# A head worked batch by batch: one batch's gates and projections ahead of the other's

## The reference, cut to what matters

```python
xn = layernorm(x)                         # x: (2, 1024, 128)
def ffn(xn):                              # attention with low-rank experts
    pooled = xn.mean(axis=1)              # one row per batch
    logits = relu(pooled @ gw1.T + gb1) @ gw2.T + gb2
    gates  = softmax(top_k(logits, 2))    # 2 of 8 experts, per batch
    W[p]   = Wm[p] + sum_e gate_e * U[p,e] diag(S[p,e]) V[p,e]    # p in q, k, v, o
    q, k, v = xn @ W[q] * SCALE, xn @ W[k], xn @ W[v]             # 16 heads of 8
    return softmax(q k^T) v @ W[o]
def attn(xn):                             # RWKV: time mixing, then channel mixing
    h = layernorm(xn); k, v, r = mix(h) @ w_tk, mix(h) @ w_tv, sigmoid(mix(h) @ w_tr)
    x1 = xn + r * wkv(k, v)               # a scan over 1024 tokens
    return x1 + sigmoid(cr @ w_cr) * (relu(ck @ w_ck)**2 @ w_cv)
out = x + attn(xn) + ffn(xn)
```

## Time and profile before

| | |
|---|---|
| median of 3 runs | 448.7 us (448.13 to 449.81) |
| the profiled execution | 447.99 us, span of its instructions 445.9 us |
| busy share of the span | PE 95%, DVE 86%, ACT 76%, POOL 43% |
| mean granted clock of PE | 0.992 of full speed |
| first place of stage A | 30.91 us |
| scores of step 0 / of step 1 | 64.63 us / 67.31 us |

### The profile page before, as it was taken

The page is one execution under the profiler, slowest core; times in us unless marked ns, Lnnn a source line. Parts: engine busy times, 40 slices in busy tenths (PEclk is TensorE's granted clock), DMA queues, the critical chain, the costliest instruction groups (busy, mean ns, idle before and its releaser), DMA issues.

```text
span 445.9 us, 8560 instructions
## 1 busy us (share of the span) xinstructions
PE 423.2 (95%) x3248; PEld 144.7 (32%) x3248; DVE 385.4 (86%) x657; ACT 340.2 (76%) x461; POOL 191.2 (43%) x271
## 2 busy tenths in 40 slices
PE   1889989999999999999999999999999999999995
PEld 1644223333233232232323223323232333322334
DVE  8578899998999997899999789999888999976354
ACT  3547837879887898788799969878986877988660
POOL 5029581935551625382353546417264611431200
PEclk9988999999999999999999999999999999999999
DMA  7004303141414141404241413332322421050301
GB/s 240 11 11 56 40 6 34 19 66 21 64 22 67 20 66 18 64 7 70 24 64 19 66 17 54 31 60 24 60 27 26 57 37 28 17 116 10 124 25 47
DMA packets 45509, 20.46 MB, mean 46 GB/s; under 512 B 36796, under 2 KB 36956, under 8 KB 45468
## 3 DMA queue, kind: packets, MB, share of 16 engines
q1 hardware_dynamic: 44486, 18.96, 27.6%
q10 hardware_dynamic: 982, 0.95, 0.6%
HBM read 4.74 MB, written 4.98 MB: 22 GB/s over the span
## 4 chain that ended last, share of the span: by engine, by line
PE 86%; DVE 9%; ACT 3%; issue 1%; DMA 1%; DVEq 0%
PE banks L1475 27%; PE banks L1462 22%; PE banks L1365 18%; PE banks L1426 8%; DVE half_max L1177 5%; PE banks L1327 3%; ACT probs L972 2%; PE banks L1333 1%; PE banks L1405 1%; PE banks L1311 1%; PE banks L1262 1%; DVE work L1204 1%; PE banks L1319 1%; PE banks L1228 1%; DVE stats L1023 1%
## 5 line engine op out<-in xcount | busy, mean ns | idle before, releaser
L1177 DVE TENSOR_REDUCE half_max<-banks 128x1 f32<-128x512 f32 x512 | 318.5, 684 | 21.2 <-PE banks L1365 19.6
L972 ACT ACTIVATE probs<-banks 128x1024 f32<-128x1024 f32 x256 | 248.2, 1023 | 51.5 <-PE banks L1462 48.3
L1475 PE MATMUL banks<-probs,v_op 128*32 128x512 f32 x1024 | 136.4, 605 | 0.4 <-ACT probs L972 0.4
L1365 PE MATMUL banks<-k_main,q_main 64*128 64x512 bf16 x512 | 117.5, 388 | 5.6 <-DVE half_max L1177 3.3
L1462 PE MATMUL banks<-q_main,k_main 64*128 64x512 bf16 x512 | 99.3, 377 | 0.4 <-ACT probs L972 0.2
L1462 PE MATMUL banks<-q_tail,k_tail 35*128 35x512 bf16 x512 | 99.3, 377 | 0.0
L1365 PEld LDWEIGHTS banks<-k_main,q_main 64*128 64x128 bf16 x512 | 36.5, 93 | 151.0 <-DVE half_max L1177 132.1
L1462 PEld LDWEIGHTS banks<-q_tail,k_tail 35*128 35x128 bf16 x512 | 27.2, 94 | 26.1
L1462 PEld LDWEIGHTS banks<-q_main,k_main 64*128 64x128 bf16 x512 | 26.4, 95 | 25.1 <-ACT probs L972 10.2
L1475 PEld LDWEIGHTS banks<-probs,v_op 128*32 128x32 f32 x1024 | 20.1, 108 | 32.5 <-issue 30.3
L718 POOL TENSOR_TENSOR work<-work 128x512 f32<-128x512 f32 x16 | 16.6, 1039 | 28.6 <-ACT work L961 28.6
(11 more groups left out here) (184 smaller groups left out, 420.5 us busy)
## 6 DMA issues: line engine op xcount, KB each, us to landing
ctx_dram<-ctx_sb SPq DMA_DIRECT2D x15, 256.0 KB, 2.1
q_main<-parts SPq DMA_DIRECT2D x60, 48.0 KB
k_main<-parts SPq DMA_DIRECT2D x60, 48.0 KB
mat_sb<-in_mats_dram SPq DMA_DIRECT2D x2, 768.0 KB, 5.3
v_op<-V SPq DMA_DIRECT2D x16, 64.0 KB, 3.9
parts<-ctx_dram SPq DMA_DIRECT2D x4, 256.0 KB, 4.4
q_main<-parts SPq DMA_DIRECT2D x30, 32.0 KB
k_main<-parts SPq DMA_DIRECT2D x30, 32.0 KB
```

The costliest lines, as they stand in the source:

```text
L972: a.activation(probs[:, (2 * step + h) % 4, :, :], banks[:, 2 * h:2 * h + 2, :], ACT.Exp).then_inc(b_read, 1)
L1177: v.tensor_reduce(half_max[:, n % 2, u:u + 1], ring_bank(at), axis=AX.X, op=ALU.max).then_inc(a_read, 1)
L1365: mm(dst, q_main[HALF * e:HALF * (e + 1), s, P * c:P * c + P], k_main[HALF * e:HALF * (e + 1), s, CHUNK * h:CHUNK * h + CHUNK], start=True ...
L1475: last = mm(banks[g:g + 32, PV_BANK, :], v_op[:, s % 2, step, e, :], probs[:, (2 * step + h) % 4, e, :], start=(step == 0), stop=True, ski ...
```

## The change: what it does

**Head.** Only batch 0 is prepared. Chunks 0 and 1 are measured and normalised first, on DVE, and each tile is transposed as soon as it is there. Batch 0's gates are computed alone, on one partition, and only its q and k weights; chunks 2 and 3 are normalised on ACT (`normalise`, 8 tiles, with a bias and a scale per token) instead of DVE. Only q and k of the first 512 tokens (banks 0 and 2) are projected, split and laid out before the first place, and bank 3 is projected.

**Pair 0's places.** Their order goes by 512 columns of keys and then by queries, so that the first eight need only the first 512 tokens of q and k, the next eight bank 3 (k), the last sixteen bank 1 (q).

**Opening.** What the head no longer does is set between the places: the rest of bank 3, all of bank 1, batch 1's gate column, the v and o weights (`weights` 0 and 1) and q's and k's weights of batch 1 (`weights` 2). Three of the nine `mixed` jobs go to the main loop, which then has six. The transposes, `late` and `values` jobs are spread anew, and the banks are assigned by a table (`FILL_BANKS`).

**Other engines.** The scaling of U moves from DVE to ACT (six of eight), the 22 small copies into `row_of` from ACT to POOL, the copies of pair 0's rows all to ACT, the constants of chunks 2 and 3 to POOL. DVE adds the main weights between its reads (`ADD_WEIGHTS`). SP loads pair 1 before pair 0's tails. The kernel computes the same.

```diff
-FILL_JOBS = {2: [("turn", 0), ("turn", 1)], 5: [("turn", 2), ("turn", 3)], 9: [("values", 0)], 12: [("values", 1)]}
-FILL_JOBS.update({15 + 2 * m: [("mixed", m)] for m in range(6)})
-FILL_JOBS.update({26: [("late", 0)], 28: [("late", 1)], 30: [("late", 2)], 31: [("late", 3)]})
-FILL_JOBS.update({38: [("mixed", 6)], 40: [("mixed", 7)], 42: [("mixed", 8)]})
-LATE_JOBS = {2: ("mixed", 9), 3: ("mixed", 10), 9: ("mixed", 11), 10: ("values", 2), 15: ("values", 3)}
-LATE_GATES = {2: 2, 12: 3}
+FILL_JOBS = {0: [("gates", 1)], 2: [("left", 3, 0), ("turn", 0)], 4: [("left", 3, 1)], 5: [("rows", 3)], 7: [("project", 1)],
+             8: [("turn", 1)], 9: [("left", 1, 0)], 11: [("left", 1, 1), ("weights", 0)], 13: [("rows", 1)], 15: [("turn", 2)],
+             17: [("weights", 1)], 19: [("mixed", 0)], 21: [("mixed", 1)], 23: [("mixed", 2)], 25: [("turn", 3)],
+             27: [("values", 0)], 29: [("values", 1)], 31: [("mixed", 3)], 33: [("mixed", 4)], 34: [("mixed", 5)],
+             36: [("weights", 2)], 38: [("late", 0)], 40: [("late", 1)], 41: [("late", 2)], 43: [("late", 3)]}
+READ_GATES, ADD_WEIGHTS = 2, {13: ((2, None),), 19: ((3, None),), 37: ((0, 1), (1, 1))}
+LATE_JOBS = {2: ("mixed", 6), 4: ("mixed", 7), 7: ("mixed", 8), 10: ("mixed", 9), 12: ("mixed", 10), 15: ("mixed", 11),
+             18: ("values", 2), 20: ("values", 3)}
+LATE_GATES = {8: 2, 16: 3}
...
 # SP
-            load_tails(0, 0)
             load_pair(1, 1)
+            load_tails(0, 0)
...
 # ACT, up to the opening
+            scale_of(0); scale_of(1)
...
+            keep_xnT(0); keep_xnT(1)
+            hidden_gates(0)
+            scale_of(2); scale_of(3)
+            act.dma_start(vb_ob[:, :, :], ...)
+            exp_gates(0)
...
+            normalise(2); normalise(3)
...
+            keep_xnT(2); keep_xnT(3)
+            part(0, 0, 0); hidden_gates(1)
+            part(0, 0, 1); exp_gates(1)
+            part(0, 0, 2); keep_rows(0); keep_rows(2)
+            part(3, 0, 0); part(3, 0, 1); part(3, 0, 2)
+            keep_h(0); keep_rows(3); scale_shift(0)
+            part(1, 0, 0); scale_shift(1); keep_h(1); part(1, 0, 1)
+            scale_u(2, 0); scale_u(2, 1)
+            part(1, 0, 2); scale_shift(2); keep_rows(1)
...
 # DVE
+            part(2, 0, 0); top_gate(1); part(2, 0, 1); compare_gates(1); part(2, 0, 2); weigh_gates(1)
...
 # PE
+            hidden_gates(0); warm(6)
+            logits_of(0); warm(20)
+            for k in range(4):
+                pe.wait_ge(xn_late, k + 1)
+                turn_x(2, (k,))
+            gate_column(0)
...
+            turn_x(3, (0, 1))          # then the weights of q and k, batch 0, and turn_x(3, (2, 3))
+            project(0); project(2)
+            take_part(0, 0); hidden_gates(1); take_part(2, 0); take_part(0, 1); logits_of(1); take_part(2, 1)
+            pair_rows(0); pair_rows(2); project(3)
...
-                if n == 0 and k == 0:
-                    pe.wait_ge(q_rows_kept, 2)
-                    pe.wait_ge(k_rows_kept, 2)
+                if n == 0 and k in (0, 8, 16):
+                    pe.wait_ge(rows_kept, 2 + k // 8)
```

More of the change, by code:

```diff
@@ L745, in _ @@
             split_max(0, 0)
+            bias_v(1)
+            take_shift(3)
             mix_tokens(3)
@@ L778, in _ @@
             act.dma_start(gw2_sb[:, :], gw2).then_inc(small_in, 16)
[L779 to L788, removed]
@@ L789, in _, with scale_of @@
-            act.dma_start(vb_ob[:, :, :], rows.rearrange("(o r) c -> o r c", o=1).to_broadcast([P, 2, C])
-            ).then_inc(rows_in, 16)
+            act.dma_start(gb2_sb[:, :], gb2).then_inc(small_in, 16)
+            act.wait_ge(consts, 2)
+            def scale_of(n):
+                of_n = slice(4 * n, 4 * n + 4)
+                act.wait_ge(moments_ready, 4 * n + 4)
+                a.activation(rstd[:, of_n], moments[:, of_n, 1], ACT.Ln, bias=eps_c[:, 0:1]).then_inc(log_var, 1)
+                act.wait_ge(log_var, n + 1)
+                a.activation(rstd[:, of_n], rstd[:, of_n], ACT.Exp, scale=-0.5).then_inc(rstd_ready, 1)
@@ new lines, in keep_xnT, with normalise @@
+            def keep_xnT(n):
+                act.wait_ge(x_transposed, n + 1)
+                a.activation(columns_of(xnT, n), bank(n), ACT.Copy, accum_out=sums[:, n:n + 1]).then_inc(xnT_ready, 1)
+            def normalise(n):
+                act.wait_ge(late_shift, n - 1)
+                for i in range(4 * n, 4 * n + 4):
+                    a.activation(xn_tok[:, i, :], x_sb[:, i, :], ACT.Identity, bias=neg_mean[:, i:i + 1],
+                                 scale=rstd[:, i:i + 1]).then_inc(xn_late, 1)
@@ L794, in _ @@
             a.activation(col("qS"), col("qS"), ACT.Copy, scale=SCALE).then_inc(q_scaled, 1)
-            def keep_xnT(n):
-                act.wait_ge(x_transposed, n + 1)
-                a.activation(columns_of(xnT, n), bank(n), ACT.Copy, accum_out=sums[:, n:n + 1]).then_inc(xnT_ready, 1)
[L801 to L806, removed]
@@ L807, in _ @@
-            act.wait_ge(shifted_ready, 1)
-            a.activation(gexp[:, :], logits[:, :], ACT.Exp, bias=neg_top[:, 0:1]).then_inc(gexp_ready, 1)
-            act.wait_ge(var2_ready, B)
+            keep_xnT(0)
+            keep_xnT(1)
+            hidden_gates(0)
+            scale_of(2)
+            scale_of(3)
+            act.dma_start(vb_ob[:, :, :], rows.rearrange("(o r) c -> o r c", o=1).to_broadcast([P, 2, C])
+            ).then_inc(rows_in, 16)
+            exp_gates(0)
+            act.wait_ge(moe_in, 16)
@@ L815, in _ @@
[L815 to L825, removed]
+            a.activation(rstd2[:, :], rstd2[:, :], ACT.Exp, scale=-0.5).then_inc(rstd2_ready, 1)
@@ L834, in part, with keep_rows, scale_u @@
                              bias=col("kb") if t else qb_s[:, 0:1]).then_inc(part_ready[j], 1)
[L836 to L843, removed]
+            def keep_rows(j):
+                t, n = part_bank(j, 0)
+                act.wait_ge(rows_ps, ROW_ORDER.index(j) + 1)
+                a.copy((k_main if t else q_main)[:, 0, CHUNK * n:CHUNK * (n + 1)], bank(j)).then_inc(rows_kept, 1)
+            def scale_u(i, b):
+                act.wait_ge(sg_ready, 2)
+                a.activation(u_s[:, i, b, :], mat("qkvo"[i] + "U"), ACT.Copy, scale=sg[:, i, b:b + 1]).then_inc(us_ready, 1)
             def keep_h(u):
@@ L857, in keep_v, with scale_shift @@
                     "p (k r w) -> p k r w", k=CHUNK // P, w=2 * HD)).then_inc(v_read, 1)
[L859 to L864, removed]
+            def scale_shift(m):
+                act.wait_ge(h_diff, m // 3 + 1)
+                a.activation(mix_slot[m], h_shift[CHUNK_ORDER[m // 3]], ACT.Copy,
+                             scale=col("mix_" + "kvr"[m % 3])).then_inc(h_scaled, 1)
             def keep_kvr(m, src):
@@ L915, in _ @@
                           max_rows[80:96, 0, :]).then_inc(max_in[0], 16)
-            for m in range(6, 9):
-                keep_kvr(m, bank(kvr_bank(m)))
+            keep_kvr(5, bank(kvr_bank(5)))
+            keep_gate(1)
+            for m in (9, 10, 11):
+                scale_shift(m)
+            for j in range(CHUNKS):
+                keep_late(j)
             weights = ((lo_u, 1.0, 0.0), (hi_u, -1.0, 0.0), (lo_y, 1.0, neg_first[:, :]), (hi_y, -1.0, col("first")))
@@ L1186, in _ @@
                 read_place(at)
+                if at == READ_GATES:
+                    scale_gates(1)
+                for i, b in ADD_WEIGHTS.get(at, ()):
+                    add_main(i, b)
             def one_step(p, step):
@@ L1269, in take_part, with pair_rows @@
                    skip_group_check=True).then_inc(left_ps[j], 1)
+            def pair_rows(j):
+                t, n = part_bank(j, 0)
+                pe.wait_ge(part_ready[j], PARTS)
+                for i in range(PARTS):
+                    last = mm(bank(j), row_of[:, t, i, :], parts[0:2 * HD, t, i, n, :], start=(i == 0),
+                              stop=(i == PARTS - 1))
+                last.then_inc(rows_ps, 1)
+            for n in range(2):
+                for k in range(4):
+                    pe.wait_ge(xn_ready, 4 * n + k + 1)
+                    turn_x(n, (k,))
@@ L1271, in _ @@
+            pe.wait_ge(neg_ident_ok, 1)
+            warm(8)
+            pe.wait_ge(small_in, 64)
+            hidden_gates(0)
+            warm(6)
+            logits_of(0)
+            warm(20)
+            for k in range(4):
+                pe.wait_ge(xn_late, k + 1)
+                turn_x(2, (k,))
+            gate_column(0)
+            pe.wait_ge(xn_late, 8)
+            turn_x(3, (0, 1))
             pe.wait_ge(moe_in, 16)
-            expert_weights(0)
-            expert_weights(1)
@@ L1274, in _ @@
-            warm(4)
+            for i in range(2):
+                pe.wait_ge(us_first, i + 1)
+                mm(bank(5 + i)[:, 0:P], mat("qk"[i] + "V"), u_s[:, i, 0, :], start=True, stop=True).then_inc(weff_ps, 1)
+            turn_x(3, (2, 3))
             pe.wait_ge(weff_ready, 1)
             project(0)
```

(25 more changed lines are left out.)

407 lines of the change are left out of this document (226 added, 181 removed).

## The result

The change made the kernel slower: 453.25 us (median of 20 runs, 450.45 to 458.93) against 449.02 (20 runs, 448.13 to 451.33), a ratio of 1.0081 [1.0058, 1.0103]. The ratio leaves out the three slowest runs of the changed kernel (457.4 to 458.9), in which the mean clock was lowest. The forecast was 448.4, with 452.2 as the upper end. The profiled execution took 453.03.

What follows compares the result with a forecast made beforehand. PE was taken to carry most of the chain of waits. From the profiled 447.99, 4.9 saved up to step 1's scores and 4.6 lost in the loop gave 447.7, with the median 0.7 above: 448.4 us, range 444.4 to 452.2.

Steps and rivals of the forecast that it cites:

- The head: Work before the first place: `project(0)` at 16.6 instead of 20.17, first place at 24.7, 6.2 us earlier.
- The opening: From first place to step 1's scores: place 16 at 36.7, scores at 62.4, giving back 1.3 of 6.2 us.
- The walk: Place-by-place pricing of ACT's and PE's streams in the opening: 12.0 us for the first sixteen places.
- The sign "after 64": End of the opening: the prediction is wrong if step 1's scores come after 64.
- the sign for the clock: Head: PE's granted clock was to read 1.00 from 10 to 24.
- The third case: Half clock in the head, falling before about 17 us: 2.8 us more, 451.2; chance 0.14.
- Transposes don't feel it: Head and opening: transposes cost the same at half clock, 0.27 at full against 0.24 at half.
- The loop: Main loop gives back 4.6 us: 3.15 for three more `mixed` jobs, 1.1 for bare scans, 0.35 for `keep_gate(3)`.
- The 0.35 for `keep_gate(3)`: Main loop: cost of moving `keep_gate(3)` from step 12 to step 16, between nothing and 0.6.
- The wait ahead of `late 0`: Opening: PE waits 0.9 us before `late 0` for the two `add_main` behind place 37.
- The late maxima: Opening: SP starts 6 us later, so maxima land late for step 0's scores; 451.5, chance 0.08.
- The even case: Whole kernel: the head's gain is paid back by jobs and bare scans, 446.5 to 450.9; chance 0.45.

Runs made afterwards that it cites:

- experiment 1: Changed kernel plus identity products, whose result nobody reads, in PE's pauses in the head; 448.14 us, 0.9973 of the kernel before.
- experiment 6: Kernel of experiment 4 with only the move of three `mixed` jobs from the opening to the main loop; 454.6 us, ratio 1.009.
- experiment 3: Changed kernel with the layout matmuls over 128 rows instead of 16, added selector rows zero; 448.27 us, ratio 0.9989.
- experiment 4: Kernel before the change with the layout matmuls over 128 rows instead of 16; 446.93 us (0.9936), in a second run 447.45 us (0.9952).
- experiment 5: Kernel before the change without its 60 identity products; 452.82 us, ratio 1.0051.
- experiments 7 and 8: Changed kernel, identity products in the head, layout over 128 rows; 7: loop jobs on steps 3 and 9, 445.85 us; 8: three `mixed` back in opening, 445.18 us.

## Why the prediction was wrong

The forecast held in its main terms but for one step, and that step carried 6 us.

- **The head: right.** `project(0)` forecast at 16.6, measured 16.52, behind ACT's eight tiles (11.9 to 14.75; 11.87 to 14.95, 0.385 apart for 0.35). The gates' first matmul came at 9.68 (9.3). First place 25.16 (24.7); in it is 0.36 of a `project(3)` that took 1.42 instead of 1.06, since the clock fell in it.
- **The opening: the step that failed**, "place 16 comes at 36.7 ... 62.4, 4.9 earlier than 67.31". The walk priced every pass, turn and layout from 24.7 on at 2.4 GHz, while the earlier trace rows of the same argument showed 1.2 GHz behind just these layouts. Measured, place 16 came at 42.81 and step 1 at 68.73: all of the loss arises before place 16. With the clock held (experiment 1) place 16 came at 36.84 and step 1 at 62.81: the walk itself was right to 0.4, and what failed was the clock that its prices took for granted. The sign "after 64" is the one that came true; the sign for the clock ended at 24, just ahead of the fall.
- **The third case named the mechanism, at the wrong place and size.** It put the fall before about 17 us and charged 2.8 for four items of the head. The clock stayed up there: `project(0)` took 1.98 / 4 = 0.50 a pass. By the rule of the Trainium skill, "TensorE: Matmul & The Clock Gate", Part 4: PE-mode transpose, that thin stretch of transposes would have throttled; the trace shows no such fall, as those 0.50 tell, but the stretch is only some 4 us behind the last identity product and holds other passes too, so it doesn't settle the rule. The clock fell at 24.3, behind the thin stretch from 18 to 22 and the first layouts, and cost 68.73 - 62.81 = 5.9 in the opening. A chance of 0.14 was too small for something that the kernel before already did, and 451.2 was too near. Its counter-argument, full clock through as thin a stretch at 8 to 14, trusted a column that is wrong there (under the hardware, below).
- **"Transposes don't feel it": wrong.** Four took 1.04 at half clock and 0.59 at full. The comparison had taken the head's 0.27 each as a price at full clock, because the record shows 1.00 there; that price was itself one at half clock (under the hardware, below).
- **The loop: right mechanism, 4.6 forecast, 3.89 measured**, and the same 3.90 for the move alone (experiment 6). Of it 0.83 were the bare scans (1.1 forecast; both on the chain), and the rest is near the 3 x 1.05 of the jobs; together 3.98. The 0.35 for `keep_gate(3)` didn't show. That the loop cost 0.7 less than forecast hides as much of the opening's loss in the total.
- **The wait ahead of `late 0`: right.** PE waits for `add_main` ahead of `late 0`: on the chain stand three reads of VectorE, 57.27 for 1.88, and the two sums, 0.41, and PE itself is idle for 1.20 of it (0.9 forecast):

```profile
59.59 1.13 PE L1445 MATMUL banks<-xnT,w_eff 128*128 128x512 f32 x2 [1.20 <-DVE w_eff L1158]
```

- **The late maxima: right.** The case of SP's late maxima fell: the chain waits for no transfer behind the load of x (DMA 1%, as in the earlier trace rows).
- **The even case is near what the schedule alone gives, in part by luck.** With the clock held it is 448.14, where the sum said 448.4; but 1.0 of that is the fall near the end, which no term had, against 0.7 that the loop cost less.
- **Slips in the sum.** The upper bounds of scans and gate add 0.5 to the 4.6 (up to 5.1) and not 1.0, so the range ended at 451.7 by its own terms. SP's margin was 1.9 and not 2.2: its terms end at 57.8, and 62.4 less 2.7 is 59.7. Neither changes the outcome.

What stays open: what of the head's thin work lets the clock fall at 24.3. Filling PE's pauses prevents the fall (experiment 1) and fuller matmuls shorten it (experiment 3); neither alone says which of the pauses or passes is decisive.

## What to carry to other kernels

Before pricing a rearranged stretch, look up the granted clock in the old one, and price the new stretch at both levels, by the durations of known forms and not by the clock's column alone: thin work behind a pause can cost more than the shorter path saves, and products that nobody reads, or operand rows of zeros, can pay for themselves. Ask of each piece of work that is moved what it cost where it stood, not only what it costs where it goes: here three products that lay hidden beside VectorE, and held the clock, went to a loop that pays for them in full.

## What the hardware showed unexpectedly

**The record of the clock says 1.00 at the start while PE works at half speed.** The kernel before, transposes in the head and in the opening (duration min/median/max, first and last start):

```profile
L1228 PE MATMUL banks<-ident,xn_tok x16: 417/421/477, 8.2 to 13.0; 128*128 128x128 f32 x16
...
L1311 PE MATMUL banks<-ident,work x16: 417/421/474, 31.9 to 36.3; 128*128 128x128 f32 x16
```

and the kernel of experiment 4 in its second run, where the opening's transposes stand at full clock, with its identity products:

```profile
L1311 PE MATMUL banks<-ident,work x16: 272/273/332, 33.1 to 36.0; 128*128 128x128 f32 x16
...
L1223 PE MATMUL banks<-neg_ident x60: 218/311/315, 13.4 to 21.7; 128*128 128x128 bf16 x60
```

The same transposes take 421 ns in the head at a recorded 1.00, 421 at a recorded 0.50, and 273 at 1.00 with PE warm. The Trainium skill, "TensorE: Matmul & The Clock Gate", Part 1: The HAM clock gate, says that the engine begins at 1.2 GHz until work has warmed it; these durations agree, and the recorded clock of this profile doesn't show it. Ahead of the first recorded fall the duration of a known form tells the clock, not the column. It is also what made experiment 5 slow: passes of 1029 ns instead of 592 between 21 and 26, at a recorded 1.00.

**The same kernel can warm up later.** In the second run of experiment 4 the first 40 identity products behind the gates took 0.11 each, up to 19.4, where the first run had them at 0.06; `project(0)` came at 21.83 instead of 20.21, and the span was 445.3 instead of 443.7.

**The length of the half clock varies from run to run.** Spans of the changed kernel that count in the ratio go from 448.6 at a mean clock of 0.984 to 453.9 at 0.970; with the clock held, the runs of experiments 7 and 8 lie between 443.1 and 446.0, at 0.992 to 1.000.
